# Seven of sixteen scan states by way of a transposition, two tiles of them in some steps

## The reference, cut to what matters

```
h_n[d, t] = exp(delta[d, t] * A[d, n]) * h_n[d, t-1] + delta[d, t] * u[d, t] * B_n[t]
y[d, t]  += sum over n of h_n[d, t] * C_n[t]
```

## Time and profile before

| what | value |
|---|---|
| median of three runs | 15,066.38 us (15,064.4 to 15,070.1) |
| span of the profiled execution | 15,072.9 us; no other time is given for it |
| TensorE (PE) busy, instructions | 13,109.8 us, 87%, 61,336 |
| VectorE (DVE) busy | 12,836.0 us, 85%, 13,813 |
| ScalarE (ACT) busy | 11,077.9 us, 73%, 22,762 |
| GpSimd (POOL) busy | 10,522.1 us, 70%, 4,198 |
| mean granted TensorE clock | 0.981 |

### The profile page before, as it was taken

One profiled execution on the slowest core, in us unless ns is written; L12 is line 12 of the kernel. 1 busy time (PEld: TensorE's weight loads), 2 busy tenths in 40 slices (PEclk: granted clock), 3 DMA queues, 4 the chain that ended last, 5 costly groups with the idle time before them and its releaser, 6 DMA issues.

```text
span 15072.9 us, 238570 instructions
## 1 busy us (share of the span) xinstructions
PE 13109.8 (87%) x61336; PEld 7880.5 (52%) x61336; DVE 12836.0 (85%) x13813; ACT 11077.9 (73%) x22762; POOL 10522.1 (70%) x4198
## 2 busy tenths in 40 slices
PE   6888988889888898888988889888898888988889
PEld 4555455554555545555455554555545555455554
DVE  8999669996799967998589985899849998499984
ACT  5887578875788757886678866788667886678866
POOL 6998069980699807997079970899608996099950
PEclk9999999999999999999999999999999999999999
DMA  3433023430334303343033420334203442043420
GB/s 112 130 129 119 20 94 127 132 109 20 99 129 138 98 20 104 130 138 91 20 113 128 137 85 20 117 129 136 81 20 121 131 134 76 20 129 129 135 69 25
DMA packets 907950, 1468.07 MB, mean 97 GB/s; under 512 B 38912, under 2 KB 891904, under 8 KB 893664
## 3 DMA queue, kind: packets, MB, share of 16 engines
q1 hardware_dynamic: 906560, 1452.37, 30.1%
HBM read 1350.07 MB, written 102.17 MB: 96 GB/s over the span
## 4 chain that ended last, share of the span: by engine, by line
issue 30%; POOL 23%; PE 20%; DVE 18%; DMA 4%; ACT 4%; DVEq 1%; POOLq 0%; SPq 0%; ACTq 0%
POOL area L1583 16%; DVE area L1085 12%; POOL area L1593 5%; PE ps L908 5%; PE ps L922 5%; DMA area<-bc_rows 4%; DVE area L1107 3%; PE ps L697 3%; ACT ps L1375 1%; PE ps L775 1%; DVE area L352 1%; POOL area L1572 1%; PE ps L758 1%; ACT ps L1334 1%; PE ps L684 1%
## 5 line engine op out<-in xcount | busy, mean ns | idle before, releaser
L1085 DVE TENSOR_TENSOR_SCAN area<-ps,hst,area 128x384 f32<-128x384 f32 x9216 | 8600.7, 1007 | 127.3 <-POOL area L1583 66.9
L1583 POOL TENSOR_TENSOR area<-area 128x1152 f32<-128x1152 f32 x3072 | 8004.4, 2641 | 50.3 <-POOL area L1572 42.2
L1375 ACT ACTIVATE ps<-area,a_neg 128x384 f32<-128x384 f32 x9216 | 5287.8, 580 | 1142.7 <-DVE area L1085 1091.6
L697 PE MATMUL ps<-area,ident 128*128 128x384 f32 x12672 | 4590.4, 499 | 844.1 <-POOL area L1593 773.2
L697 PEld LDWEIGHTS ps<-area,ident 128*128 128x128 f32 x12672 | 2271.1, 192 | 2554.3 <-POOL area L1593 970.3
L684 PE MATMUL ps<-ident,area 128*128 128x128 f32 x17280 | 2425.9, 277 | 6.0 <-ACT area L1342 6.0
L1567 POOL TENSOR_TENSOR area<-area,ones 128x2304 f32<-128x2304 f32 x8 | 43.6, 5453 | 3348.3 <-ACT area L1298 3227.7
L1526 ACT ACTIVATE area<-ps,t_neg,area 128x768 f32<-128x768 f32 x1728 | 1617.8, 986 | 922.6 <-PE ps L908 922.6
L684 PEld LDWEIGHTS ps<-ident,area 128*128 128x128 f32 x17280 | 2198.7, 194 | 60.2 <-ACT area L1342 10.9
L1342 ACT ACTIVATE area<-ps,area 128x384 f32<-128x384 f32 x2880 | 1637.3, 569 | 544.3 <-PE ps L675 542.2
L1593 POOL TENSOR_TENSOR area<-area 128x1152 f32<-128x1152 f32 x768 | 2026.2, 2638 | 1.8 <-ACT hst L1318 1.8
(11 more groups left out here) (139 smaller groups left out, 9976.7 us busy)
## 6 DMA issues: line engine op xcount, KB each, us to landing
area<-bc_rows SPq DMA_DIRECT2D x1536, 768.0 KB, 6.7
xz<-x_normed SPq DMA_DIRECT2D x144, 288.0 KB, 6.2
area<-in_x SPq DMA_DIRECT2D x18, 1728.0 KB, 10.6
area<-x_padded SPq DMA_DIRECT2D x24, 1250.0 KB, 5.7
z_raw<-z_st SPq DMA_DIRECT2D x144, 192.0 KB, 6.2
area<-z_raw SPq DMA_DIRECT2D x8, 3456.0 KB, 15.2
x_padded<-x_st SPq DMA_DIRECT2D x120, 200.0 KB, 7.7
x_normed<-area SPq DMA_DIRECT2D x9, 1728.0 KB, 7.9
```

What stands on the lines that cost most here:

```text
L697: m = e.matmul(ps[:, 5 + j, 0:CH], ident[:], hb[:, i % NH, j], start=i == 0, stop=i == N - 1)
L1085: e.tensor_tensor_scan(rev(hb[:, i % NH, j], k), rev(ps[:, 2 + j, 0:CH], k), rev(dbu[:, i % NH, j], k), hst[:, i, j:j + 1], ALU.mult, ALU. ...
L1375: e.activation(ps[:, 2 + j, 0:CH], dlt[:, par, j], ACT.Exp, scale=a_neg[:, j, k, i:i + 1]).then_inc(da, 1)
L1583: e.tensor_tensor(dbu[:, i % NH], du[:, par], row_b[:, q % 2, i % ROWS:i % ROWS + 1].broadcast_to([128, J, CH]), ALU.mult).then_inc(dbus, 1)
```

## The change

Seven states are turned instead of five: 1, 3, 6, 7, 10, 12, 13 instead of 1, 4, 7, 10, 13. GpSimd keeps the product with C of states 0, 4 and 9 (before 0, 3, 6, 9), VectorE of 2, 5, 8, 11, 14, 15 (before also 12). That makes 21 turned tiles per step instead of 15 and nine state sums instead of eleven. Where a slot had at most one turned tile, a table TURN_AT now gives a slot one or two. Of two, ScalarE multiplies the first behind the exponential of j = 0 and the second behind that of j = 2 (a single one stays behind j = 1); TensorE turns the first at the usual place, and turns the second at the end of the slot, after the sums of VectorE's states. The turned sum is issued as a transposition. The unit at m = 14 waits for the product of state 11 instead of 12.

```diff
-POOL_N = (0, 3, 6, 9)
-TURN_N = (1, 4, 7, 10, 13)
+POOL_N = (0, 4, 9)
+TURN_N = (1, 3, 6, 7, 10, 12, 13)
+TURN_AT = {2: (0,), 3: (1, 2), 4: (3, 4), 5: (5,), 7: (6, 7), 8: (8, 9), 9: (10, 11), 11: (12, 13), 12: (14,),
+           13: (15, 16), 14: (17, 18), 15: (19, 20)}
-SUM_AT = {0: 3, 2: 4, 3: 6, 5: 7, 6: 9, 8: 10, 9: 12, 11: 13, 12: 14, 14: 16, 15: 17}
+SUM_AT = {0: 3, 2: 4, 4: 7, 5: 7, 8: 10, 9: 12, 11: 13, 14: 16, 15: 17}
...
                     for j in range(J):
                         i = e.matmul(ps[:, 5 + j, tt * 128:(tt + 1) * 128], ht[:, tt, j * 128:(j + 1) * 128], ident[:],
-                                     start=False, stop=False)
+                                     start=False, stop=False, is_transpose=True)
...
-                    if turn_at(m):
-                        turn(g, m)
-                    if turn_at(m - 1):
-                        turned_sum(g, m - 1)
+                    now, before = turns(m), turns(m - 1)
+                    if now:
+                        turn(g, now[0])
+                    if before:
+                        turned_sum(g, before[-1])
                     for i in SUM_ORDER:
                         if SUM_AT[i] == m and i in DVE_N:
                             state_sum(g, i)
+                    if len(now) == 2:
+                        turn(g, now[1])
+                        turned_sum(g, now[0])
...
-                    e.wait_ge(hcs, gd + (1 + DVE_N.index((8, 12)[i]) + 1))
+                    e.wait_ge(hcs, gd + (1 + DVE_N.index((8, 11)[i]) + 1))
...
+                def turned_products(g, k, c, m, j):
+
+                    now = turns(m)
+                    if len(now) == 1 and j == 1:
+                        turned_product(g, k, c, now[0])
+                    if len(now) == 2 and j != 1:
+                        turned_product(g, k, c, now[j // 2])
```

More of the change, by code:

```diff
@@ L411, in rev, with turns @@
             return ap if k < 2 else ap[:, ::-1]
[L413 to L418, removed]
+        def turns(m):
+            return TURN_AT.get(m, ())
         def ct_group(q):
@@ L666, in scan_phase, with turn @@
                 e.wait_ge(ct_cp, b * GM + 3)
-                def turn(g, m):
-                    n, at, tt = turn_at(m)
+                def turn(g, at):
+                    n, tt = TURN_N[at // 3], at % 3
                     if tt == 0:
@@ L677, in turn, with turned_sum @@
                     i.then_inc(turn_mm, 1)
-                def turned_sum(g, m):
-                    n, at, tt = turn_at(m)
+                def turned_sum(g, at):
+                    tt = at % 3
                     e.wait_ge(turn_cp, g * NT + (NT + at + 1))
@@ L1334, in c_copy, with turned_product @@
                     e.activation(ps[:, 1, 0:CH], row_c[:, q % 2, i % ROWS], ACT.Copy).then_inc(c_ps, 1)
-                def turned_product(g, k, c, m):
-                    n, at, tt = turn_at(m)
+                def turned_product(g, k, c, at):
+                    n, tt = TURN_N[at // 3], at % 3
                     t = c * 3 if k < 2 else (NC - 1) * 3 - c * 3
@@ L1384, in body @@
                                 store_y(g - 1, *last, j + 1)
[L1385 to L1388, removed]
+                            if i > 0:
+                                turned_products(g, k, c, i - 1, j)
+                            elif last:
+                                turned_products(g - 1, *last, N - 1, j)
                         if i == 0 and last:
@@ L1414, in scan_phase @@
                 c_copy(g, N - 1, None)
-                turned_product(g, K - 1, NC - 1, N - 1)
-                turned_product(g, K - 1, NC - 1, N)
+                for at in turns(N - 1):
+                    turned_product(g, K - 1, NC - 1, at)
                 for j in range(J):
```

## The result

The changed kernel takes 15,372.4 us (median of four runs, 15,369.0 to 15,377.7), the kernel before 15,067.6 us (four runs beside them). The ratio is 1.0203, with a 95% interval of 1.0191 to 1.0216: slower by 305 us, where 88 us were forecast.

The account below looks back on a forecast made before the run. VectorE, at 52.54 us a step, was to replace GpSimd as the bound; waits of 1.36 + 0.14 + 0.3 + 0.1 and 0.65 for half clock gave 55.09, or 15,155 us for the run; range 14,980 to 15,430.

Parts of the forecast that it names:

- The sign: Whole run: the changed kernel would be slower, by 0.46 us a step or 88 us.
- the bound: Chunk step: VectorE, at 52.54 us, becomes the last engine in place of GpSimd, which falls from 54.63 to 52.04.
- the waits of slot 7: Slot 7: ScalarE and VectorE wait behind TensorE's sums and turns, so state 9 starts late, 1.36 us in every step.
- the clock term: Pause before slot 7: TensorE falls to half clock in one step in three, 1.48 us each, taken as 0.5 a step.
- The row in slot 7: TensorE in slot 7: delta tile, sum of state 4, then turn of tile A, in sequence; 1.36 us a step.
- Other waits: Odd directions' copies of y 0.14, pairs in slots 13 and 14 0.3, small waits elsewhere 0.1 us a step.
- The turned sum of three instructions: TensorE's turned sums: transposed, each should take 3 instructions and 0.33 us, at worst the old 0.67.
- the case of half clock in every step: Slot 7 alone: 1.48 us more in each step on 54.44, upper end of the forecast's own range, 15,315.
- The other 0.15 for the clock: Pauses between the pairs of slots 14 to 16: half clock there costs 0.15 us a step.
- The second: Rival: waits come as placed in every step but the clock stays as before; 54.44 us a step, 15,030; chance 0.24.
- The first: Rival: ScalarE's wait in slot 7 costs nothing and the clock holds; 53.0 us a step, 14,750; chance 0.10.
- The third: Rival: clock falls at several places, slots 7 to 9 and 14 to 16, nearly every step; 57.4 us, 15,600; chance 0.14.

## Why the prediction was right and wrong

The sign, the bound and the waits of slot 7 were right; the clock term was too small by a factor of almost four, and that is nearly all of the difference.

- **The bound.** VectorE at 52.54 us a step in place of GpSimd: right. Where the row in slot 7 is gone, the third step of an image takes 52.88 us and the fourth direction 52.80 in the mean. GpSimd has left the chain (1%). One reading on the way was too wide: the 773.2 of 844.1 us are a part of the idle time before the state sums; TensorE's whole idle time is 13% of the span, 1,963 us.
- **The row in slot 7 at full clock, 1.36 us.** Right, piece by piece. In the 41 full-clock steps: delta tile at 1.38 (forecast 1.38), sum at 2.13 (2.13), turn at 4.07 (4.07), product A at 4.60 (4.60), second scan of state 8 at 5.69 (5.73), state 9 at 8.46 (8.51). As a price: 54.67 us a step with products in the pause against 53.32 without the row, 1.35. One wait in it was not named: the first scan of state 8 stands for the sum of state 4. At full clock it starts at 4.36, against 3.99 where the row is gone; in the steps at half clock this is the longest wait of all.
- **Other waits, 0.14 + 0.3 + 0.1 = 0.54.** About right in sum, not in place. Measured by the scans' starts in the kernel with the products: state 0 0.24 (not foreseen), state 15 0.14 (0.56 in k = 1 alone, for slots 13 and 14), states 3 and 6 about 0.1; together 0.5. The one before state 0 is a wait of VectorE's product of state 14 for ScalarE's copy of its C row: 0.20 to 0.24 us in the three directions that have a unit, none in the fourth.
- **The turned sum of three instructions**: right, 12,096 records of 275 ns for 4,032 tiles. The prediction let 0.67 instead of 0.33 cost little ("lies in the range"). With plain sums the changed kernel took 15,492.7 us, outside the stated range, though fewer of its steps were at half clock; in the version with the sum of state 4 in slot 6 they cost 1.20 us a step.
- **The clock term.** This is the step that failed: "one step in three, 0.5", from 1.48 us each. Both factors were too small. Half clock came in 143 of 184 steps, 0.78 instead of 0.33. And it cost 2.45 instead of 1.48, because not one sum but the whole row runs slow: in the step shown the delta tile holds TensorE 0.69 longer, the sum 1.91, the turn 0.27. The 1.48 was read from a sum of which only a part ran slow: where it starts, the clock was still at 1.00, as the line below shows (columns of the earlier trace rows). A sum that is at half clock throughout is 4.05 long. 0.78 x 2.45 = 1.90 us a step where 0.5 stood; even the case of half clock in every step, 15,315, lay below the measured time. The other 0.15 for the clock, between the pairs, did not show as a stall of VectorE.

```profile
936.00:936.50 0.50, 0.38 (x1) 0.30 (x2) 0.50 (x2) 0.50 (x2) 0.50 (x1) 1.00 0.60 203
```

- **The sum.** 52.54 + 1.30 (state 9 at full clock, 8.46 - 7.16) + 1.90 + 0.5 = 56.24, measured 56.57. Of the rest, 0.2 is the first step of an image, which is 61.14 long (56.81 before) and counts once in 23; 0.1 is not accounted for.
- **The rivals.** The second (waits as placed, clock as before, 15,030) is what the run with products showed, at 15,029.7, but that the times agree so closely is luck: the rival gave 0.19 us to each of 192 steps, 36 us, while the spans show 7 us from the 184 steps, 24 from the last steps of the images and 15 from the parts between them. The point it named, half clock in fewer than one step in eight, was passed far in the changed kernel. The first (no waits, 14,750) is nearly what moving one sum gave, 14,784. The third had the clock falling often, which came, but at the wrong price and for a reason that fell: in slots 8, 9 and 14 to 16 no stall of VectorE came from it, and 18 transposes in the pause held the clock.

## What to carry to other kernels

When an edit takes work off an engine that does not bound, read what stood in its place: the emptied slot is a pause, and where the clock falls in a pause in front of a row that sets the end, everything in the row can run at half clock, not one instruction alone (2.45 us here, not 1.48). Price such a pause as the share of steps that are hit times the whole row, and first try to move needed work into it; here one number in a table made 1.020 of the time before into 0.981. What a cheaper instruction is worth depends on who is last: the transposed sum gave nothing behind GpSimd and 242 us once VectorE was the bound.

## What the runs showed of the hardware

- The length of the pause just in front does not decide the clock by itself: the same 2.56 us was followed by 0.50 in one step (866.56) and by 1.00 in another (2201.46). How much TensorE did in the pause moves the share of steps at half clock: 143, 78 and 0 of 184 with nothing, one product and three products added. Which steps are hit goes by their place in the image (above); what sets it was not tried.
- Transposes of float32, put into that pause, hold the granted clock at 1.00 as products do (18 of them in 2.13 us a step, 0 of 184 steps at half clock). Transposes alone, without products around them, were not tried.
- A sum in PSUM by transposition takes three instructions of 275 ns for a tile of 384 channels where the product with the identity takes six of 277.
